# K and V projections that contract 128 + 64 context columns in five products instead of 96 + 96 in six

## The reference

```python
q = (x @ Wq)        # x: 16 x 112 x 256, layer-normed
k = (context @ Wk)  # context: 16 x 375 x 192, Wk, Wv: 192 x 256
v = (context @ Wv)
scores = einsum('bhid,bhjd->bhij', q, k) * scale   # 16 heads of 16 columns
attn = softmax(scores); out = einsum('bhij,bhjd->bhid', attn, v)
x = x + tanh(g_xattn[0]) * (out @ Wo)
```

## Time and profile before

| | |
|---|---|
| runs | 614.09, 614.59, 615.00 us, median 614.59 |
| profiled execution | 619.51 us, span 617.8 us, mean granted clock 0.908 |
| PE busy | 496.9 us, 80% of the span, 4738 instructions |
| PEld busy | 448.0 us, 73% |
| DVE busy | 429.3 us, 69%, 906 instructions |
| ACT busy | 334.8 us, 54% |
| POOL busy | 289.9 us, 47% |
| K products (L533) | 192, 52.6 us |
| V products (L543) | 288, 64.5 us |
| DMA | 68974 packets, 74.88 MB |

### The profile page before, as it was taken

How to read it: one execution, slowest core, us unless ns; L and a number is a source line. 1 busy time by engine, 2 the same in 40 slices (tenths; PEclk the granted TensorE clock), 3 DMA queues, 4 the chain that set the end, 5 groups by cost and what they waited for, 6 DMA issues and landing times. The chain is left out here.

```text
span 617.8 us, 15147 instructions
## 1 busy us (share of the span) xinstructions
PE 496.9 (80%) x4738; PEld 448.0 (73%) x4739; DVE 429.3 (69%) x906; ACT 334.8 (54%) x623; POOL 289.9 (47%) x251
## 2 busy tenths in 40 slices
PE   2477798999999999999989933198879999999930
PEld 2366687888888888888877832087869999999930
DVE  1745578999899898999998558577785555545520
ACT  2232265766667666666765565176676555455420
POOL 9400365445555654545566320333465655666340
PEclk9997689999999999999996565589999999999985
DMA  8336745566455645546330349865543434433234
GB/s 186 94 82 169 164 111 117 163 171 164 114 153 135 158 105 160 162 102 167 90 87 1 99 141 307 260 189 134 141 88 60 70 61 68 64 55 60 28 42 127
DMA packets 68974, 74.88 MB, mean 121 GB/s; under 512 B 28696, under 2 KB 57200, under 8 KB 68736
## 3 DMA queue, kind: packets, MB, share of 16 engines
q1 hardware_dynamic: 60864, 63.22, 38.7%
q0 software_dynamic: 8064, 11.06, 11.1%
HBM read 42.51 MB, written 14.98 MB: 93 GB/s over the span
## 5 line engine op out<-in xcount | busy, mean ns | idle before, releaser
L343 POOL TENSOR_TENSOR PL<-PT 125x448 f16<-125x448 f32 x96 | 99.8, 1041 | 134.5 <-ACT PT L459 134.4
L723 DVE TENSOR_REDUCE mx<-bank 112x1 f32<-112x375 f32 x256 | 130.9, 543 | 28.2 <-PE bank L557 26.9
L459 ACT ACTIVATE PT<-bank 125x448 f32<-125x448 f32 x192 | 103.8, 544 | 84.8 <-PE bank L572 84.0
L1312 POOL DMA_INDIRECT acc_scr<-ys,slot_row x42 | 68.7, 1637 | 83.3 <-ACT ys L1352 74.4
L557 PE MATMUL bank<-KS,QS 97*112 97x376 f32 x256 | 91.8, 381 | 13.0 <-DVE mx L723 10.5
L572 PE MATMUL bank<-QS,KS 98*125 98x256 f32 x384 | 87.1, 313 | 3.1 <-DMA QS<-nm 2.3
L572 PEld LDWEIGHTS bank<-QS,KS 98*125 98x125 f32 x384 | 69.5, 202 | 4.3 <-DMA QS<-nm 2.5
L1386 PE MATMUL bank<-xH,GH 128*128 128x256 f16 x336 | 64.8, 275 | 8.1 <-ACT sg L1337 7.8
L557 PEld LDWEIGHTS bank<-KS,QS 97*112 97x112 f32 x256 | 46.2, 185 | 25.6 <-DVE mx L723 21.8
L1386 PE MATMUL bank<-xL,GH 128*128 128x256 f16 x336 | 64.6, 274 | 0.0
L1386 PE MATMUL bank<-xH,GL 128*128 128x256 f16 x336 | 64.4, 273 | 0.0
(11 more groups left out here) (213 smaller groups left out, 1088.5 us busy)
## 6 DMA issues: line engine op xcount, KB each, us to landing
KS<-kH SPq DMA_DIRECT2D x128, 94.0 KB, 2.2
KS<-kL SPq DMA_DIRECT2D x64, 94.0 KB, 2.1
QS<-q_scr SPq DMA_DIRECT2D x96, 56.0 KB
ctx_sb<-in_ctx SPq DMA_DIRECT2D x16, 281.2 KB
wsq<-in_L_ffn_gate_w SPq DMA_DIRECT2D x8, 512.0 KB, 3.7
wsq<-in_L_ffn_up_w SPq DMA_DIRECT2D x8, 512.0 KB, 4.4
w_raw<-in_L_ffn_gate_w SPq DMA_DIRECT2D x8, 512.0 KB, 4.8
w_raw<-in_L_ffn_up_w SPq DMA_DIRECT2D x8, 512.0 KB, 4.2
```

The source lines that it names most:

```text
L343: pool.tensor_tensor(PL[:, 2 * k:2 * k + 2, :, 0:N], PT[:, 2 * k:2 * k + 2, :, 0:N], PH[:, 2 * k:2 * k + 2, :, 0:N], ALU.subtract).then_in ...
L459: act.activation(PT[:, 2 * k:2 * k + 2, :, 0:N].rearrange("p a e i -> p (a e) i"), psST[k % 2][0:JP].rearrange("p (a i) -> p a i", i=NI)[: ...
L723: dve.tensor_reduce(mx[:, hd:hd + 1], psS[hd % 2][0:N, 0:M], AX.X, ALU.max).then_inc(v_max, 1)
L1312: pool.indirect_dma_start(acc_scr, bass.IndirectOffsetOnAxis(ap=slot[:, TH * t + k:TH * t + k + 1].bitcast(U32), axis=0), ys[:, u, k, :], ...
```

## The change

Wk and Wv are held as 128 rows and a rest of 64. The rest stands twice, in partitions 0 to 63 and 64 to 127 of the second half, so each weight is loaded by three DMAs. The context is laid out in 256 columns, the last 64 of them a copy of columns 128 to 191 that a second DMA brings; so the transposes deliver the rest in partitions 0 to 63 and again in 64 to 127. ScalarE copies all of it as the high part. VectorE then makes the low part of the first 128 columns into `cTL`, and, in a second instruction, replaces the lower copy of the rest (partitions 64 to 127 of `cTH`) by its low part. One product over 128 rows with the stacked high weight then gives high by high and high by low of the rest at once, and one over 64 rows gives the low weight by the high context. With three products for the first 128 columns these are five. The q parts `qH` and `qL` are kept for two groups instead of four, and the copy of group g waits for the stores of group g - 2.

```diff
-        shapes = {"q": (Wq, 128), "k": (Wk, CK), "v": (Wv, CK), "o": (Wo, 128)}
+        shapes = {"q": (Wq, 128), "k": (Wk, 128), "v": (Wv, 128), "o": (Wo, 128)}
+        REST = CTX - 128
-        cTH = sb("cTH", [CK, 2, MP], F32R)
-        cTL = sb("cTL", [CK, 2, MP], F32R)
+        cTH = sb("cTH", [128, 2, MP], F32R)
+        cTL = sb("cTL", [128, MP], F32R)
...
-        qH = first("qH", [128, GROUPS, 2, GB * N], F32R)
-        qL = first("qL", [128, GROUPS, 2, GB * N], F32R)
+        qH = first("qH", [128, 2, 2, GB * N], F32R)
+        qL = first("qL", [128, 2, 2, GB * N], F32R)
...
-                    sp.dma_start(ctx_sb[:, u, :, :], ctx_768[bass.ds(b, 1), :, :].rearrange("o (p t) d -> p (o t) d", t=JT)
-                                 ).then_inc(d_ctx[u], 16)
+                    rows = ctx_768[bass.ds(b, 1), :, :].rearrange("o (p t) d -> p (o t) d", t=JT)
+                    sp.dma_start(ctx_sb[:, u, :, 0:CTX], rows).then_inc(d_ctx[u], 16)
+                    sp.dma_start(ctx_sb[:, u, :, CTX:256], rows[:, :, 128:CTX]).then_inc(d_ctx[u], 16)
...
-                    sp.dma_start(Wf[k][:], w.rearrange("(c p) n -> p c n", p=p)).then_inc(s_w[k], 16)
+                    sp.dma_start(Wf[k][:, 0, :], w[0:128, :]).then_inc(s_w[k], 16)
+                    for half in range(2):
+                        sp.dma_start(Wf[k][REST * half:REST * (half + 1), 1, :], w[128:CTX, :]).then_inc(s_w[k], 16)
...
+                    if g >= 2:
+                        act.wait_ge(s_qw[g - 2], 64)
...
+                def stacked(k):
+
+                    H, L = WH[k], WL[k]
+                    return [(H[:, 0, :], cTH[:, 0, :]), (L[:, 0, :], cTH[:, 0, :]), (H[:, 0, :], cTL[:]),
+                            (H[:, 1, :], cTH[:, 1, :]), (L[0:REST, 1, :], cTH[0:REST, 1, :])]
...
-                    for n, (w, r) in enumerate(((WH, cTH), (WL, cTH), (WH, cTL))):
-                        for k in range(2):
-                            mm = pe.matmul(misc[:, 512 * m:512 * m + MP], w["k"][:, k, m * 128:(m + 1) * 128],
-                                           r[:, k, :], start=(n == 0 and k == 0), stop=(n == 2 and k == 1))
+                    for n, (w, r) in enumerate(stacked("k")):
+                        mm = pe.matmul(misc[:, 512 * m:512 * m + MP], w[:, m * 128:(m + 1) * 128], r,
+                                       start=(n == 0), stop=(n == 4))
...
+                    for n, (w, r) in enumerate(stacked("v")):
+                        mm = pe.matmul(misc[0:JP, DIM * t:DIM * (t + 1)], r[:, JP * t:JP * (t + 1)], w,
+                                       start=(n == 0), stop=(n == 4))
...
-                    dve.tensor_tensor(cTL[:, :, 0:M], misc[0:CK].rearrange("p (c n) -> p c n", c=2)[:, :, 0:M],
-                                      f32(cTH[:, :, 0:M]), ALU.subtract).then_inc(v_T, 1)
+                    dve.tensor_tensor(cTL[:, 0:M], misc[:, 0:M], f32(cTH[:, 0, 0:M]), ALU.subtract)
+                    dve.tensor_tensor(cTH[REST:128, 1, 0:M], misc[REST:128, 512:512 + M], f32(cTH[REST:128, 1, 0:M]),
+                                      ALU.subtract).then_inc(v_T, 1)
```

More of the change, by code:

```diff
@@ L110, in attention @@
         VS = sb("VS", [JP, NB, JT, HEADS, VW], BF16)
-        ctx_sb = sb("ctx_sb", [JP, NB, JT, CTX], F32)
+        ctx_sb = sb("ctx_sb", [JP, NB, JT, 256], F32)
         kH = sb("kH", [128, NB, 2, MP], F32R)
@@ L234, in wait @@
                 eng.wait_ge(s, value)
-        constants = [(f32(cTH[:, :, M:MP]), 0.0), (f32(cTL[:, :, M:MP]), 0.0), (bias_sb[:, M:MP], 0.0),
+        constants = [(f32(cTH[:, :, M:MP]), 0.0), (f32(cTL[:, M:MP]), 0.0), (bias_sb[:, M:MP], 0.0),
                      (VS[:, :, :, :, VW - 1:VW].rearrange("p u t h o -> p (u t) h o"), 1.0)]
@@ L396, in transposed @@
                         wait(act, p_V, JT * b)
[L397 removed]
+                        act.activation(cTH[:, :, 0:M], misc[:].rearrange("p (c n) -> p c n", c=2)[:, :, 0:M],
                                        ACT.Copy).then_inc(a_T, 1)
@@ L481, in w_high @@
                 def w_high(k):
-                    act.wait_ge(s_w[k], 16)
+                    act.wait_ge(s_w[k], 48 if k in "kv" else 16)
                     act.activation(WH[k][:], Wf[k][:], ACT.Copy, scale=SCALE if k == "q" else 1.0).then_inc(s_wh, 1)
@@ L518, in ctx_T @@
                     b, h, u = at(i, c)
-                    pe.wait_ge(d_ctx[u], 16 * (h + 1))
+                    pe.wait_ge(d_ctx[u], 32 * (h + 1))
                     wait(pe, a_V, b)
@@ L540, in project_v @@
                         pe.wait_ge(v_K, b + 1)
-                    for n, (w, r) in enumerate(((WH, cTH), (WL, cTH), (WH, cTL))):
-                        for k in range(2):
-                            mm = pe.matmul(misc[0:JP, DIM * t:DIM * (t + 1)], r[:, k, JP * t:JP * (t + 1)],
-                                           w["v"][:, k, :], start=(n == 0 and k == 0), stop=(n == 2 and k == 1))
+                    for n, (w, r) in enumerate(stacked("v")):
+                        mm = pe.matmul(misc[0:JP, DIM * t:DIM * (t + 1)], r[:, JP * t:JP * (t + 1)], w,
+                                       start=(n == 0), stop=(n == 4))
                     mm.then_inc(p_V, 1)
@@ L840, in q_low @@
                     for c in range(2):
-                        ins = dve.tensor_tensor(qL[:, g, c, :], (psS, psST)[g % 2][c][:, 0:GB * N],
-                                                f32(qH[:, g, c, :]), ALU.subtract)
+                        ins = dve.tensor_tensor(qL[:, g % 2, c, :], (psS, psST)[g % 2][c][:, 0:GB * N],
+                                                f32(qH[:, g % 2, c, :]), ALU.subtract)
                     ins.then_inc(s_ql, 1)
```

10 lines of the change are left out of this document (5 added, 5 removed).

## The result

The changed kernel takes 672.53 us (median of four runs, 672.21 to 674.18). The kernel before, run on the same chip, takes 614.34 (612.78 to 615.0). The ratio is 1.093, with a 95% interval of 1.088 to 1.099: slower, by more than anything that the prediction allowed for. It had forecast 610.8 and a range of 606.8 to 615.4. A run more than 1.5% above its kernel's fastest counts in the median and not in the ratio.

What follows compares the result with a forecast made beforehand. Neither TensorE nor VectorE alone was taken to bound the loop; they hand work to each other across two banks. Terms -6.5 - 0.8 + 3.0 - 0.6 + 0.7 + 0.4 = -3.8 us gave 610.8 us, range 606.8 to 615.4.

Steps and rivals of the forecast that it cites:

- So I take the row count as free.: Loop's K and V products: 128 rows cost no more than 96; a step loses 0.70 us of TensorE work.
- Rival (e): K and V products: 128 rows cost more, as much as the sixth product, saving no TensorE time; 618.7 us, chance 0.03.
- TensorE's work and the step shrink together: Attention loop: TensorE's busy share stays near 0.92, so the granted clock was expected to stay 1.00.
- Rival (f): Attention loop: granted clock falls; even one step at the lower level adds 8 us, giving 619; chance 0.03.
- The gain of 0.50 a step: Loop, contexts 3 to 15: 0.53 us gained at the thirteenth maximum less 0.03; 13 steps give -6.5 us.
- The extra VectorE instruction, +0.03: Loop's low part as two instructions of 375 columns, not one of 750: 0.03 us a step, bounds 0 and 0.30.
- X later by 3.0: Program start: five more DMAs ahead of X and smaller packets make X land 3.0 us later, delaying layer norm.
- SyncE's first step, +0.4: First loop step: one more context DMA ahead of the row of maxima on gapless SyncE costs 0.4 us.
- V of context 0, -0.6: Start, at the low clock: three V products less, with x's transposes following without idle time, save 0.6 us.
- q buffers, +0.7: Start: ScalarE's q copy of group 3 waits for group 1's stores; stall 0 to 1.2 us, taken as 0.7.
- products 160 and 240: Sign in the profile after: K and V products number 160 and 240 instead of 192 and 288.
- the loop term: Attention loop: steps of 17.3 us instead of 17.8, VectorE's score waits some 0.6 us a step; -6.5 us over 13 steps.

## Why the prediction was wrong, point by point

- **"So I take the row count as free."** This is the step that failed. It was argued from products of 96 and 128 rows, and the one row count that the change brings in, 64, has no row in the trace of before. An unseen case was priced from seen ones at a single value, without a bound of its own. The rows show 0.29 lost per K block and 0.28 per V block, 1.42 us a step against the 0.70 to be gained, and the run with 64 rows in the kernel before (ratio 1.089) shows that this alone makes the 9%. Rival (e) had the right place ("the change saves no TensorE time") for the wrong reason, stopped at zero saving, and had a chance of 0.03.
- **"TensorE's work and the step shrink together"**, clock 1.00. Rival (f) asked about it and priced one step of lower clock at 8 us, with a chance of 0.03. The clock fell in ten of the 13 steps, to 0.91 in the mean, each time behind a wait of some 1.3 us. With the centring it is worth 2.1 us a step in the one profile that tells them apart, the larger part of the loss. A step was taken as a sum of durations that stay as they are; the duration of the centring depends on what GpSimd does beside it.
- **The gain of 0.50 a step.** The wait that was to go went; its worth to the step was wrong. The kernel with five products and no other edit loses the waits as forecast (12.6 to 5.5 us), and its 13 steps are 0.4 us shorter, not 6.5. The step followed ended at the thirteenth maximum; what comes after it (the centring, the clock, the weighted sums that wait for VectorE) took the gain.
- **The extra VectorE instruction, +0.03.** The two low-part instructions of the kernel after start at 212.46 and 213.02, and the next operation at 213.60: 1.14 us together, not the 0.92 looked for, against 0.86 before. That is 0.28 more, close to the upper bound of 0.30, and 3.6 us over 13 steps if VectorE were the later engine throughout; what it costs by itself was not tried.
- **X later by 3.0.** It came at 20.61 us instead of 16.95: 3.7. In the kernel with the loads alone 2.5. The term holds, its working only in part: issuing X itself came 3.9 us later (6.10 for 2.18), not 2.0, since the additional issues took 0.55 to 0.95 us each and not 0.40.
- **SyncE's first step, +0.4.** Mis-sized: the row of maxima came 3.2 us later behind the context DMA (15.7 for 12.5), and as much later in the kernel with the loads alone. The queries behind the added DMA were taken as unchanged, and they took 1.9 more. Put at 3.2, this term would have made the sum -1.0 instead of -3.8, no difference that can be measured. In the kernel after, most of it is hidden behind TensorE's own delay; in the kernel with the loads alone it is not, and that one costs some 10 us.
- **V of context 0, -0.6.** The three products less brought no gain. With three switches to 64 rows at the low clock the block took 4.95 us, about 0.8 more than before.
- **q buffers, +0.7.** No stall. The copy of group 3 came at 60.86 and waited for TensorE alone (1.42 us); the later start had given the stores their time.
- **What it named to look for** served well: products 160 and 240 (right, 64 less in view), statistics near 20 us (right), and "steps unchanged or VectorE's waits unchanged would prove the loop term wrong", which the first table shows.

## What to carry to other kernels

Before a layout is changed to save a product, look in the trace for the exact shape that it brings in, and where there is none, keep that price open to both sides; here 64 rows among larger products cost 0.28 us each time at full clock, and 72 nothing, so padding the rows is the cheaper form. Price a DMA by one of the same pattern, and with the queue behind it. A step in which two engines hand work to each other gives back only what the next wait leaves, and where an operation's duration depends on its neighbour on GpSimd, a shift of a few tenths of a microsecond can cost more than the work that was saved.

## What the runs showed of the hardware that I had not expected

- A product of 64 rows between products of more rows loses the overlap of weight loads on both sides: distances of 0.26 and 0.37 us for 0.17 (376 columns), 0.21 and 0.31 for 0.12 (256 columns). With 72 rows the distances are 0.17 and 0.18, and the kernels with 72, 96 and 128 rows took 625, 630 and 627 us; a second product of 64 rows next to the first added nothing to the loss. That 64 is the exact limit was not tried, nor were fewer rows or the upper ones.
- VectorE's centring, an SBUF to SBUF operation of 0.34 us, took 1.53 to 1.61 us beside GpSimd's rounding of V in the kernel after, and ended 0.14 us after it.
- A wait of TensorE of 1.32 us in a step that was busy otherwise stood ahead of 6 us at 0.50 of the clock, and ten of 13 steps had such a fall; in the profile with the wait gone the loop was at 0.99, gaps and all.
- With products of 64 rows the clock stood at 0.50 through 14 us (90 to 104) in which TensorE was busy without a pause, with the loads of the change and with those of before (13.88 us busy).
- A context DMA split in two took 1.6 us to issue for 0.74 ahead of the first step, and the six query DMAs behind it 5.0 us for 3.1; in the loop these six took 4.1 to 5.4 us, and 2.7 to 3.8 before.
